# Keys of 8-wide heads spread by ACT instead of by transfers, and value matmuls on four quarters of the array, in a four-layer gated cross-attention kernel

## What is computed

```python
x = x + tanh(g_xattn[0]) * L0_xattn(layernorm(x), ctx)   # 16 heads of 64, 4 key/value heads
x = x + tanh(g_ffn[0])   * L0_ffn(layernorm(x))          # self attention, 16 heads of 8, + 8 experts, top 2
x = x + tanh(g_xattn[1]) * L1_xattn(layernorm(x), ctx)   # 16 heads of 8, padding mask
x = x + tanh(g_ffn[1])   * L1_ffn(layernorm(x))          # shared expert + 7 routed, top 2
x = x + tanh(g_xattn[2]) * L2_xattn(layernorm(x), ctx)   # 4 heads of 32, rotary
x = x + tanh(g_ffn[2])   * L2_ffn(layernorm(x))          # 8 experts, top 1
x = x + tanh(g_xattn[3]) * L3_xattn(layernorm(x), ctx)   # 16 heads of 64
x = x + tanh(g_ffn[3])   * L3_ffn(layernorm(x))          # gated channel mix
```

## Time and profile before

| | |
|---|---|
| median of 3 runs | 4557.56 us (4556.44 to 4560.14) |
| profiled execution | 4552.95 us |
| its span | 4551.1 us |
| mean granted clock of the matmul engine | 0.866 of 2.4 GHz |
| busy: matmuls, DVE, ACT, POOL | 87%, 66%, 38%, 17% |

### The profile page before, as it was taken

How to read it: one execution, slowest core, us unless ns; L and a number is a source line. 1 busy time by engine, 2 the same in 40 slices (tenths; PEclk the granted TensorE clock), 3 DMA queues, 4 the chain that set the end, 5 groups by cost and what they waited for, 6 DMA issues and landing times.

```text
span 4551.1 us, 105680 instructions
## 1 busy us (share of the span) xinstructions
PE 3947.3 (87%) x36890; PEld 3104.3 (68%) x36890; DVE 3006.2 (66%) x9082; ACT 1735.9 (38%) x4156; POOL 764.9 (17%) x575
## 2 busy tenths in 40 slices
PE   6999978888886888889999999777737899999965
PEld 4888855555554555589999999655537777777754
DVE  4666657777775777766666666799861355555569
ACT  3555534444442344333333333222203344444421
POOL 1222221111110000011111111100171122222211
PEclk9999987777776677689999999888758999999975
DMA  3000010000001000000000000100015200000000
GB/s 124 8 7 8 7 23 6 6 6 6 6 7 65 16 16 15 15 6 0 0 0 0 0 0 3 44 12 12 6 39 191 98 12 12 9 12 12 10 13 26
DMA packets 102053, 97.04 MB, mean 21 GB/s; under 512 B 31664, under 2 KB 91056, under 8 KB 101296
## 3 DMA queue, kind: packets, MB, share of 16 engines
q1 hardware_dynamic: 97408, 76.94, 5.6%
q0 software_dynamic: 4096, 8.40, 0.6%
q10 hardware_dynamic: 432, 10.19, 0.6%
HBM read 46.97 MB, written 19.66 MB: 15 GB/s over the span
## 4 chain that ended last, share of the span: by engine, by line
PE 60%; DVE 18%; SPq 8%; issue 7%; POOL 2%; DMA 2%; ACT 1%; DVEq 1%; POOLq 0%; ACTq 0%
PE ps L768 54%; SPq L591 7%; PE ps L936 5%; DVE acc L1658 2%; DMA arena_a<-kT 1%; DVE o_sb L1637 1%; POOL scr L718 1%; PE ps L806 1%; DVE arena_b L1606 1%; POOL route L740 1%; DVE xn L1442 1%; DVE x_sb L1557 1%; DVE st L1401 1%; DVE mx L1527 1%; DVE vsmall L1614 1%
## 5 line engine op out<-in xcount | busy, mean ns | idle before, releaser
L768 PE MATMUL ps<-xcT,small 128*128 128x256 f32 x2176 | 610.1, 419 | 34.7 <-DMA xcT<-in_ctxT 25.4
L732 POOL TENSOR_TENSOR rstd<-veps,neghalf 128x2 f32<-128x2 f32 (+1 forms) x224 | 167.9, 749 | 2403.8 <-DVE veps L1434 2071.2
L768 PEld LDWEIGHTS ps<-xcT,small 128*128 128x128 f32 x2176 | 411.3, 204 | 233.3 <-issue 114.5
L768 PE MATMUL ps<-arena_b,qT 64*64 64x64 f32 (+3 forms) x11136 | 541.8, 242 | 21.6 <-DVE arena_b L1606 20.3
L1278 ACT ACTIVATE kT<-ps 128x256 f32<-128x256 f32 (+1 forms) x768 | 294.4, 383 | 623.6 <-PE ps L768 547.4
L768 PE MATMUL ps<-small,xcT 128*64 128x64 f32 (+5 forms) x3072 | 482.7, 384 | 51.4 <-DVE acc L1658 30.3
L768 PE MATMUL ps<-xhi,parts_a 128*128 128x256 f32 (+1 forms) x2112 | 500.4, 289 | 22.7 <-DVE qT L1687 22.7
L768 PEld LDWEIGHTS ps<-arena_b,qT 64*64 64x64 f32 (+3 forms) x11136 | 463.5, 149 | 58.4 <-issue 35.0
L1248 ACT ACTIVATE pT<-ps 128x512 f32<-128x512 f32 (+1 forms) x576 | 303.3, 571 | 467.0 <-PE ps L936 465.3
L1687 DVE TENSOR_TENSOR qT<-kT,ps 128x256 f32<-128x256 f32 (+1 forms) x768 | 316.8, 419 | 188.5 <-ACT kT L1278 181.0
L768 PE MATMUL ps<-xlo,parts_a 128*128 128x256 f32 (+1 forms) x1536 | 430.6, 280 | 0.0
(11 more groups left out here) (212 smaller groups left out, 6388.5 us busy)
## 6 DMA issues: line engine op xcount, KB each, us to landing
wbuf<-parts_b SPq DMA_DIRECT2D x39, 512.0 KB, 3.0
arena_a<-kT SPq DMA_DIRECT2D x1024, 8.0 KB
xcT<-in_ctxT SPq DMA_DIRECT2D x96, 128.0 KB, 2.1
xn<-scr SPq DMA_DIRECT2D x39, 128.0 KB, 2.2
scr_y<-acc SPq DMA_DIRECT2D x39, 128.0 KB, 2.9
scr<-vsmall SPq DMA_DIRECT2D x9, 512.0 KB, 13.3
ctx_sb<-in_ctx SPq DMA_DIRECT2D x32, 128.0 KB, 2.1
arena_a<-in_w ACTq DMA_DIRECT2D x1, 4096.0 KB, 12.4
```

What stands on the lines that cost most here:

```text
L732: pool.tensor_tensor(rstd[:, 0:n], veps[:, 0:n], neghalf[:, 0:n], ALU.pow).then_inc(s_rstd.sem, 1)
L768: return nc.tensor.matmul(o, lhsT, rhs, start=start, stop=stop, skip_group_check=True)
```

## The change

For the 8-wide heads ACT makes eight evictions of the key bank, one for each position h of `k_spread`, with a scale for each partition (1 on head h's and head h + 8's partitions, 0 elsewhere) and a bias masked in the same way. Heads 0 to 7 lie in the lower 64 partitions, heads 8 to 15 in the upper. The scores read the same 512 columns for both halves. The 16 transfers, their semaphores and waits, and the two memsets of arena_a go. DVE computes the masks once, at the start of L0F.

For the 64-wide heads the four matmuls of a chunk go to the four quarters of the array (input half by output half). A sequence's features thus end in swapped partition halves for the second sequence of a tile. ACT evicts each bank in two parts of 64 partitions, and W runs for each sequence by itself, the second with output weights whose halves are swapped; those are loaded by two transfers before L0X and two before L3X.

```diff
+        own_head = sb("own_head", [P, 8])
+        head_bias = sb("head_bias", [P, 2, 8])
+        wo_swapped = arena_b[:, 6144:7168]
         def k_spread(par):
-            return arena_a[:, par * 4096:(par + 1) * 4096].rearrange("p (h t) -> p h t", h=16)
+            return arena_a[:, par * 4096:par * 4096 + 8 * GT].rearrange("p (h t) -> p h t", h=8)
...
+            def swap_wo(src, a, b):
+                for half in range(2):
+                    sp.dma_start(wo_swapped[half * S:(half + 1) * S, :],
+                                 src[(1 - half) * S:(2 - half) * S, a:b]).then_inc(s_swap, 16)
             sp.dma_start(small[:, 0:FIRST_W], small_in[:, 0:FIRST_W]).then_inc(s_small, 16)
+            swap_wo(small_in, *SMALL_AT["l0x_wo"])
...
-                if item == ("QK", 0):
-                    sp.wait_ge(drained[layer.front_ring.bank(g, 1)], layer.front_ring.count(g, 1))
-                    for h in range(16):
-                        sp.dma_start(k_spread(g.par)[8 * h:8 * h + 8, h, :],
-                                     kT[8 * h:8 * h + 8, g.par, :]).then_inc(s_kspread.sem(g), 16)
...
                 sp.wait_ge(s_lo, 16)
+                a = LATE.index("l3x_wo") * 1024
+                swap_wo(late_in, a, a + 1024)
                 load_tile(0)
...
-                    pool.memset(arena_a[:, 0:4096], 0.0).then_inc(s_zero, 1)
...
-                blocks = [(0, hb) for hb in range(2)] if layer is L0X else [(i, hb) for i in range(4) for hb in range(2)]
-                for turn in ((0, 1), (1, 0)):
...
+                n = 2 if layer is L0X else 8
+                for c, half, hb in itertools.product(range(n), range(2), range(2)):
+                    rows = slice(half * S, (half + 1) * S)
+                    to = slice((half ^ hb) * S, ((half ^ hb) + 1) * S)
+                    w0, heads = 512 // n, 8 // n
+                    last = mm(bank(banks[half])[to, c * w0:(c + 1) * w0],
+                              v_heads(layer, g.par)[rows, 2 * t + hb, c, :],
+                              pT[rows, t, c * heads:(c + 1) * heads, hb * S:(hb + 1) * S])
...
-                        if layer in (L0F, L1X):
-                            pe.wait_ge(s_kspread.sem(g), s_kspread.all(g))
...
+                    if chunks == 8:
+                        for c in range(8):
+                            for hb in range(2):
+                                toks = slice(hb * S, (hb + 1) * S)
+                                wo = w(layer.name + "_wo") if hb == 0 else wo_swapped
+                                last = mm(bank(b)[toks, 0:D], oT[:, t, c, toks], wo[:, c * D:(c + 1) * D],
+                                          start=c == 0, stop=c == 7)
...
-                    nc.scalar.activation(kT[:, g.par, :], bank(b)[:, GT:2 * GT], ACT.Identity,
-                                         bias=w(layer.name + "_bk")).then_inc(drained[b], 1)
+                    for h in range(8):
+                        last = nc.scalar.activation(k_spread(g.par)[:, h, :], bank(b)[:, GT:2 * GT], ACT.Identity,
+                                                    bias=head_bias[:, layer.n - 1, h:h + 1],
+                                                    scale=own_head[:, h:h + 1])
+                    last.then_inc(drained[b], 1)
...
-                        nc.scalar.activation(o, i, ACT.Copy).then_inc(drained[b], 1)
+                        for hb in range(2):
+                            rows = slice((j ^ hb) * S, ((j ^ hb) + 1) * S)
+                            last = nc.scalar.activation(oT[rows, t, :, hb * S:(hb + 1) * S],
+                                                        bank(b)[rows, :].rearrange("p (c q) -> p c q", q=S), ACT.Copy)
+                        last.then_inc(drained[b], 1)
...
-                    dve.memset(arena_a[:, 4096:8192], 0.0).then_inc(s_zero, 1)
...
+                    dve.tensor_reduce(den[:, 0, 0:16], ident.rearrange("p (h d) -> p h d", d=8), AX_X,
+                                      ALU.add).then_inc(s_heads0, 1)
+                    dve.tensor_tensor(own_head[:, :], den[:, 0, 0:8], den[:, 0, 8:16], ALU.add).then_inc(s_heads0, 1)
+                    for i, bk in enumerate(("l0f_bk", "l1x_bk")):
+                        dve.tensor_scalar(head_bias[:, i, :], own_head[:, :], w(bk), None, ALU.mult).then_inc(s_heads, 1)
```

More of the change, by code:

```diff
@@ L12 @@
+import itertools
 from contextlib import ExitStack
@@ L381, in build @@
         m_spare, m_zero, m_total, m_pad = sem("m_spare"), sem("m_zero"), sem("m_total"), sem("m_pad")
+        s_heads = ctx.enter_context(nc.semaphore("s_heads"))
+        s_heads0 = ctx.enter_context(nc.semaphore("s_heads0"))
         s_small = ctx.enter_context(nc.semaphore("s_small"))
@@ L527, in _ @@
                 sp.sem_inc(s.sem, s.credit)
-            for s in (s_ctx, s_kspread):
+            for s in (s_ctx,):
                 for i in range(2):
@@ L666, in start @@
             def start(layer):
-                if layer is L0F:
-                    for b in L0X.body_banks:
-                        pool.wait_ge(drained[b], bank_base[1][b])
-                    pool.memset(arena_a[:, 0:4096], 0.0).then_inc(s_zero, 1)
                 if layer is L2X:
@@ L772, in start @@
                     pe.wait_ge(s_small, 16)
+                    pe.wait_ge(s_swap, 32)
                     pe.wait_ge(s_const, 3)
@@ L783, in start @@
                     pe.wait_ge(s_late, 16)
+                    pe.wait_ge(s_swap, 64)
                     pe.wait_ge(m_out, TILES2)
@@ L860, in heads_times_values @@
                 pe.sem_inc(s_ready, 1)
-                blocks = [(0, hb) for hb in range(2)] if layer is L0X else [(i, hb) for i in range(4) for hb in range(2)]
-                for turn in ((0, 1), (1, 0)):
[L863 to L873, removed]
-                                          v_heads(layer, g.par)[rows, 2 * t + hb, 4 * j + i, :],
-                                          pT[rows, t, 4 * j + i, hb * S:(hb + 1) * S])
-                            if turn == (1, 0) and (i, hb) == blocks[-1]:
-                                last.then_inc(filled[banks[j]], 1)
+                n = 2 if layer is L0X else 8
[6 more added lines that the diff above has]
+                              pT[rows, t, c * heads:(c + 1) * heads, hb * S:(hb + 1) * S])
+                    if (c, hb) == (n - 1, 1):
+                        last.then_inc(filled[banks[half]], 1)
             def do(layer, item, g):
@@ L905, in do @@
                                           qT[rows, g.par, 0, t * P + hb * S:t * P + (hb + 1) * S],
-                                          k_spread(g.par)[rows, 8 * half:8 * half + 8,
-                                                          t * P + hb * S:t * P + (hb + 1) * S])
+                                          k_spread(g.par)[rows, :, t * P + hb * S:t * P + (hb + 1) * S])
                     if layer is L2X:
@@ L976, in do @@
                     b = take(ring, g, u)
+                    if chunks == 8:
[5 more added lines that the diff above has]
+                                          start=c == 0, stop=c == 7)
+                        last.then_inc(filled[b], 1)
+                        return
                     for c in range(chunks):
@@ L1154, in start @@
                 if layer is L0F:
-                    act.wait_ge(s_zero, 2)
+                    act.wait_ge(s_heads, 2)
                     act.wait_ge(s_rest, 16)
@@ L1191, in do @@
                     b = wait_filled(fr, g, u)
-                    act.wait_ge(s_kspread.sem(g.back(2)), s_kspread.all(g.back(2)))
                     nc.scalar.activation(qT[:, g.par, 0, :], bank(b, GT), ACT.Identity,
                                          bias=w(layer.name + "_bq"))
-                    nc.scalar.activation(kT[:, g.par, :], bank(b)[:, GT:2 * GT], ACT.Identity,
-                                         bias=w(layer.name + "_bk")).then_inc(drained[b], 1)
+                    for h in range(8):
[3 more added lines that the diff above has]
+                    last.then_inc(drained[b], 1)
                 elif kind == "V" and layer in (L0X, L3X):
@@ L1253, in do @@
                         b = wait_filled(ring, g, u + j)
-                        if layer is L0X:
-                            o = oT[:, t, 4 * j:4 * j + 4, :].rearrange("p i (b q) -> p b i q", b=2)
-                            i = bank(b).rearrange("p (b i q) -> p b i q", b=2, i=4)
-                        else:
-                            o = oT[:, t, 4 * j:4 * j + 4, :].rearrange("p c t -> p (c t)")
-                            i = bank(b)
-                        nc.scalar.activation(o, i, ACT.Copy).then_inc(drained[b], 1)
+                        for hb in range(2):
[3 more added lines that the diff above has]
+                        last.then_inc(drained[b], 1)
                 elif kind == "X":
@@ L1343, in start @@
                 if layer is L0F:
-                    dve.memset(arena_a[:, 4096:8192], 0.0).then_inc(s_zero, 1)
```

(2 more changed lines are left out.)

7 lines of the change are left out of this document (4 added, 3 removed).

## The result

The changed kernel takes 4602.43 us (median of 4 runs, 4599.72 to 4605.59), the kernel before 4558.85 (4 runs, 4556.44 to 4560.16). The ratio is 1.0096, with a 95% interval of 1.0079 to 1.0114. The forecast was 4586.

A forecast was written before the change was run, and what follows sets the result against it. Matmul time was taken to bound layer 0's and 3's cross attention, and the 8-wide-head stages to run partly at 1.2 GHz. Terms -22 - 44 - 3 - 15 + 4 + 98 + 10 = +28 gave 4581, from the median 4586 us; own range 4545 to 4630.

The forecast's parts named there:

- L0X with the start: Layer 0's cross attention and its edges: faster value matmuls -22 us, memset gone -3, weight transfers +2.
- L0F: Layer 0's second half: projection delayed by key evictions, mostly covered; 0.3 us a group, bounds 0 and 0.85, 10 us.
- L1X: Layer 1's cross attention: ACT's delay and lost high clock cost 3.15 us a group, +98 us; edges -15.
- The transfers' wait: Layer 1's score block waits 0.94 and 0.86 us a group for the key transfers; this goes, -0.9 us.
- the earlier rise: Layer 1's cross attention: clock rises earlier as unbroken work starts 0.9 us earlier; 0.3 us a group gained.
- L3X: Layer 3's cross attention: faster value matmuls gain 1.4 us a group, bounds 0.5 and 1.7, 44 us over 31.
- The score row: Profile row of the score block, 64 matmuls on four quarters in 1.16 us, against the value block's 2.08.
- Swaps before L3X: Two transfers of swapped output weights ahead of the routed experts: +2 us, bounds 0 and 6.
- the clock holds: Rival, layer 1: the group costs only the 0.65 us of ACT's order, 20 us; 4498 us in all, chance 0.25.
- the transfers were worth more: Rival, layer 1: free second pointer and earlier clock rise gain 1 us a group; about 4443 us, chance 0.08.
- the matmuls stay two at a time: Rival, 64-wide stages: value blocks stay at 1.95 and 2.08 us; 4652 us, chance 0.02.
- the four-part matmuls bring nothing: Rival, 64-wide stages: ACT's doubled evictions hold the banks, the 66 us are not there; 4652 us, chance 0.10.

The follow-up runs named there:

- values_only: Kernel before plus only the four-part value matmuls, swapped output weights and split evictions; keys still spread by transfers: 4518.9 us, ratio 0.991.
- keys_only: Kernel before plus only the key spread by ACT, value matmuls as before: 4639.69 us, ratio 1.018.
- filled_gap3: Changed kernel with three matmuls nobody reads put into layer 1's idle spell of 2.65 us: 4527.55 us, ratio 0.993 to the kernel before.
- moved_buffers: Kernel before with only the key spread's two small buffers (96 bytes a partition) declared and not used: 4549.11 us, ratio 0.9973.
- split_filled: split_keys with one matmul nobody reads in layer 1's idle 0.83 us: 4455.09 us, ratio 0.9767 to the kernel before.
- split_keys: Changed kernel with four of layer 1's eight key evictions moved behind pT's two evictions: 4493.98 us, ratio 0.9857 to the kernel before.
- filled_gap: Changed kernel with five matmuls nobody reads put into layer 1's idle spell of 2.65 us: 4649.5 us, ratio 1.0198 to the kernel before.

## Why the prediction was right, point by point

The sign, the place and, in the main, the mechanism were as forecast; the time came out 16 us above it, within the forecast's own range. The place of the high stretch in a group of L1X was mis-sized, and the sum for L1X came near partly because errors offset each other. By terms, on the profiled executions (predicted, then measured by the table):

- *L0X with the start* (groups -22, memset -3, transfers +2): -23, measured -7.7. The group gave 0.45, not 0.7. The first value block's gain was lost to xcT's eviction as foreseen (a gap of 0.63 us against the 0.5 or more named). The second block waits 0.22 us for four evictions (0.1 was taken), an output block lasts 1.90 to the next where it was 1.78 (0.12 lost, 0.1 taken), and each of the two new gaps also costs 0.07 of overlap between blocks. The edges took another 7 us, because four evictions in a row have nothing beside them there. The start took 2.3 us for the two transfers, 2 taken.
- *L0F* +10, measured +8.2. The steady groups hardly moved (92.22 for these four, 23.21 over ten groups, before 23.04). The wait of 0.94 us that the keys' evictions put before a projection is there in group after group and mostly covered. The clock fell here too, from 0.74 to 0.70 over the stage, and TensorE was busy for 673 us instead of 627, nearly all of it in time that it had idled. values_only took 4 us more in this stage without touching it, so the 8 us are not all the keys'.
- *L1X* -15 + 98 = +83, measured +90.0. By group from the earlier trace rows: the value block starts 0.99 later after the scores, where 1.55 less 0.3 was predicted. The transfers' wait of 0.94 is gone, as predicted. The value block is 3.22 longer, where I had taken 2.8 of at most 3.25, and 0.28 more comes from the blocks behind it, which I had left at their old clock. 0.99 - 0.94 + 3.22 + 0.28 = 3.55 for this group; the mean is 20.38 - 16.91 = 3.47, predicted 3.15. Over 31 groups 3.47 is 108 us, so the edges gave 18, where I had 15. The mis-sized step was the earlier rise, which I had priced as 0.3 us gained and not as high clock taken from the value block. The rise came 3.0 us earlier after the scores (2.0 in the mean of 24 groups), and the fall with it. That shortened the projection (1.55 us instead of 2.07) and let the key evictions start 3.88 us after the scores instead of 4.40, so pT's came at 7.47 and not at 8.1. It also took more than half of the value block's high clock, all of which I had put down to ACT's delay. The terms are not independent either: steady groups take 17.0 us before and in values_only, and 20.5 us after and in keys_only, though keys_only's value block is 6.53 us and not 6.98. That they add up to a tenth is no proof of each. filled_gap3 shows by experiment what the clock is worth.
- *L3X* -44, measured -35.5. The group gave 1.36, predicted 1.4: the value block is 1.16 us and the second block lost 0.58 where I had 0.3, since the four evictions took 2.28 us, not 2.07. The score row was the right price for the value block. The missing 7 us are at the edges again.
- *Swaps before L3X* +2, measured +4.1 for the stages from L2X. *L1F* 0, measured -9.6: not foreseen, and moved_buffers shows why.

The rivals: that the clock holds (4498) was wrong in what the change does. It priced the clock in L1X at 98 - 20 = 78 us; in filled_gap3 L1X became 91 us shorter and the kernel 75. That the transfers were worth more (4443) fell: the evictions with two pointers start 0.45 apart, not 0.37, and L1X lost 90 us. Its sum starts from -86 where its terms give -22 - 44 - 3 - 15 = -84, so it should have come out 2 us higher. That the matmuls stay two at a time fell by the value blocks, 1.09 us in L0X and 1.16 in L3X. That the four-part matmuls bring nothing fell by values_only. Its mechanism, the doubled evictions, was real: it took back 39 us, about as much as was left of the matmuls' gain. I underpriced it by counting steady groups alone and by taking the overlapped pair's rate for half-partition evictions.

## What to carry to other kernels

Ask of a new instruction what is queued behind it on its engine: eight evictions cost 81 us in front of a latency-bound one and gain time when four of them stand behind it. Where a stage's matmuls run partly at 1.2 GHz, count a delay twice, once as time and once as the work that leaves the high stretch, and ask where in the group that stretch will lie. An idle spell can be filled with matmuls nobody reads: that gave back 75 us here, an order that shortens the spell gave 108, and filling what was left of it another 39. When matmuls are packed, choose their banks by what the eviction needs, and leave the number of evictions as it was.

## What the runs showed of the hardware that was not expected

- The high stretch was 6.8 us long in the kernels before and after, and 10.2 us with one filler (split_filled) or three (filled_gap3); the low time between two stretches went from 10.2 to 13.6 us, and steady groups from 17.0 to 20.5.
- Matmuls of different rows of quarters wrote one PSUM bank at 1.16 us a block of 64, as fast as in two banks.
- An idle spell of 0.83 us in a group of 17 us, filled with one matmul, was worth 39 us over 32 groups (split_filled against split_keys).
- Buffers moved by 96 bytes a partition made matmuls of 288 and 280 ns take 286 and 277, 8 us in one stage.
- A change of some instructions in one loop went with 86 us of added time in a stage with untouched code two layers later (filled_gap), with 13 waits of 2.4 to 3.0 us that each begin 0.1 to 0.3 us after a packet of the instruction queue has started. In the middle of that stage the queue moved 103 packets of 16 KB, and none in the changed kernel.
- Half the partitions save no time: an eviction of 64x512 takes 0.590 us, as long as one of 128x512 at 0.596. Eight with a bias and a scale pointer start 0.45 apart (3.75 less one of 0.58, over 7), by the 0.46 taken.
